# A decoder layer's softmax maxima: mask and maximum products in the two 64-row halves of the array, maxima laid out by DMAs

## What is computed

```python
scores = jnp.where(causal[None, None], scores, -jnp.inf)
attn = jax.nn.softmax(scores, axis=-1)
out = jnp.einsum('bhqk,bkhd->bqhd', attn, V).reshape(b, s, H * hd)
...
scores = jnp.where(mask == 0, jnp.asarray(NEG, dtype=scores.dtype), scores)
attn = jax.nn.softmax(scores, axis=-1)
out = jnp.einsum('bhqk,bhkd->bhqd', attn, value)
```

## Time and profile before

| what | us |
|---|---|
| median of 3 timed runs | 645.84 (641.83 to 646.57) |
| span of the profiled execution | 642.8 |
| PE busy in it | 560.4 (87%) |
| DVE busy | 522.3 (81%) |
| ACT busy | 283.7 (44%) |
| POOL busy | 237.0 (37%) |
| a steady slot (300.33 to 334.69) | 34.36 |

### The profile page before, as it was taken

How to read it: one execution, slowest core, us unless ns; L and a number is a source line. 1 busy time by engine, 2 the same in 40 slices (tenths; PEclk the granted TensorE clock), 3 DMA queues, 4 the chain that set the end, 5 groups by cost and what they waited for, 6 DMA issues and landing times.

```text
span 642.8 us, 15987 instructions
## 1 busy us (share of the span) xinstructions
PE 560.4 (87%) x5410; PEld 355.3 (55%) x5410; DVE 522.3 (81%) x1443; ACT 283.7 (44%) x671; POOL 237.0 (37%) x312
## 2 busy tenths in 40 slices
PE   4576688779989999999999998998999998887884
PEld 3344445445656576666566665565566664454543
DVE  4577867777898988989898989576989987788995
ACT  1232225445635445455454554454445454434412
POOL 5323234347124262515342525344262616232211
PEclk9988789998999999999999998998999999999999
DMA  7175453644364263536354454546262636230000
GB/s 232 32 218 152 123 137 97 196 110 130 90 182 103 81 177 92 163 91 187 84 157 121 122 155 110 161 111 170 75 179 82 163 80 178 57 112 16 24 8 25
DMA packets 75808, 76.95 MB, mean 120 GB/s; under 512 B 13056, under 2 KB 67280, under 8 KB 75728
## 3 DMA queue, kind: packets, MB, share of 16 engines
q1 hardware_dynamic: 73488, 73.58, 41.4%
q10 hardware_dynamic: 2240, 2.35, 1.2%
HBM read 39.72 MB, written 27.00 MB: 104 GB/s over the span
## 4 chain that ended last, share of the span: by engine, by line
PE 57%; DVE 20%; issue 9%; DMA 4%; POOL 4%; ACT 3%; SPq 2%; DVEq 0%; POOLq 0%; ACTq 0%
PE misc L2256 14%; PE prob L2190 7%; PE misc L2242 6%; PE xpv L2231 5%; DVE junk L1447 5%; PE score L2176 4%; PE prob L2185 4%; PE misc L2342 4%; PE misc L2284 4%; PE misc L2297 2%; DVE xden L1486 2%; PE apv L2219 2%; PE score L2152 1%; POOL move_x L728 1%; DMA xden<-xoT 1%
## 5 line engine op out<-in xcount | busy, mean ns | idle before, releaser
L1447 DVE CUSTOM_DVE_ANT_0 junk<-score,maskbias 112x375 bf16<-112x375 f32 x256 | 129.1, 543 | 38.3 <-PE score L2176 38.2
L947 ACT ACTIVATE xP<-prob 128x448 f32<-128x448 f32 (+1 forms) x192 | 93.9, 540 | 66.2 <-PE prob L2190 66.0
L728 POOL TENSOR_TENSOR move_x<-mT,negeye 16x448 bf16<-16x448 f32 x64 | 63.5, 1008 | 70.2 <-ACT mT L907 70.2
L728 POOL TENSOR_TENSOR move_a<-mT,negeye 16x448 bf16<-16x448 f32 x64 | 63.1, 1009 | 62.8 <-ACT mT L907 62.8
L2256 PE MATMUL misc<-wguT,xqT 128*128 128x352 f32 x224 | 75.0, 463 | 1.9 <-ACT xqT L907 1.1
L748 POOL TENSOR_TENSOR aattT<-anum,aden 128x224 f32<-128x224 f32 x16 | 10.9, 679 | 139.0 <-DVE aden L1486 121.1
L752 POOL TENSOR_TENSOR rstd<-veps,half 128x1 f32<-128x1 f32 (+1 forms) x44 | 28.1, 639 | 89.8 <-DVE veps L1522 89.8
L2284 PE MATMUL misc<-ctxT_s,xwkT_s 128*128 128x375 f32 x128 | 50.8, 521 | 7.9 <-DVE bq_s L1405 6.7
L2176 PE MATMUL score<-xK,xQ 64*128 64x375 f16 x256 | 43.2, 331 | 16.5 <-DVE xmax L1447 16.0
L2190 PE MATMUL prob<-move_x,shift_x 128*128 128x448 bf16 x192 | 53.7, 361 | 0.1
L2256 PEld LDWEIGHTS misc<-wguT,xqT 128*128 128x128 f32 x224 | 41.8, 190 | 21.6 <-DVE hb L1570 1.8
(11 more groups left out here) (157 smaller groups left out, 1092.2 us busy)
## 6 DMA issues: line engine op xcount, KB each, us to landing
xk_dram<-xk_parts SPq DMA_DIRECT2D x64, 192.0 KB, 3.2
xK<-xk_dram SPq DMA_DIRECT2D x16, 768.0 KB, 4.6
ctxT_s<-in_ctxT SPq DMA_DIRECT2D x15, 375.0 KB, 3.6
aq_dram<-aq_parts SPq DMA_DIRECT2D x64, 64.0 KB, 2.6
ak_dram<-ak_parts SPq DMA_DIRECT2D x64, 64.0 KB, 2.1
aQ<-aq_dram SPq DMA_DIRECT2D x16, 256.0 KB, 2.9
aK<-ak_dram SPq DMA_DIRECT2D x16, 256.0 KB, 2.9
xq_dram<-xq_parts SPq DMA_DIRECT2D x64, 64.0 KB, 2.1
```

The costliest lines, as they stand in the source:

```text
L728: pool.tensor_tensor(dst[0:H, heads, :], mT[:, n].unsqueeze(1).to_broadcast([H, GH, S]), negeye[:, heads].unsqueeze(2).to_broadcast([H, GH ...
L947: act.activation(xP[0:KEYS[c], g % 2, c], prob[m][0:KEYS[c], 0:GH * S].rearrange("p (h q) -> p h q", h=GH), ACT.Exp).then_inc(probs.taken[ ...
L1447: dve.tensor_tensor_reduce(junk[:, m], score[m][0:S, 0:SC], maskbias[:], 1.0, -3.0e38, ALU.add, ALU.max, xmax[:, b.par, h:h + 1]).then_inc ...
```

## The change

The maxima are no longer spread into a block diagonal. `amax` and `xmax` get a layout in which the four heads of a group lie at rows 0 to 3 of one half and those of the next group at rows 64 to 67, for each of two pairs of groups (`BIG`). `turn_max` turns each pair of groups by a product of its own, with 128 weight columns. ACT copies 128x224 numbers with the sign turned, as bf16. A new function `flatten` makes ACT wait for its own copy and issue two DMAs, one for each half of the array: each takes four rows of `mT` and lays them one behind another into a single row of `move` (row 0 or row 64, 1,792 bytes). The semaphores `adiag_ready` and `xdiag_ready` now count the DMAs (32 a batch), and both halves and all four groups are awaited before the first shift product.

The queries are in two sets of 56 (`j`). `shift` and `move` hold in each half of 64 rows: ones (or the maxima) in rows 0 to 3, and the mask (or the unit matrix) for the 56 queries of a set in the next 56 rows. In place of two products with 128 rows and 448 columns, `turned` issues four with 64 rows and 224 columns, of which each writes every other group of 56 columns of its bank. POOL's `diagonal` and all its calls go. `flatten` stands behind each call of `maxima` in ACT's order.

At the start the tables `move_a`, `move_x`, `amax` and `xmax` are written in the first part of POOL's preparations, ahead of the semaphore `consts` (now 24), and not behind it. The mask for `shift_x` is loaded by two DMAs into `hqT`, which POOL clears first.

```diff
@@ load_mask (SP)
-                sp.dma_start(mask_t_i[H:P, :], mask).then_inc(w_mask, 16)
+                sp.wait_ge(mask_clear, 1)
+                sp.nop(nofuse=True)
+                for a in range(2):
+                    lo = HALF * a + GH
+                    sp.dma_start(mask_t_i[lo:lo + HS].rearrange("p (j s) -> p j s", j=2),
+                                 mask.rearrange("(j q) s -> q j s", j=2)).then_inc(w_mask, 16)
@@ prep (POOL)
-                for tile in (ident, identb, causal4, shift_a, negeye):
+                pool.memset(mask_t_i, 0).then_inc(mask_clear, 1)
+                for tile in (ident, identb, causal4, shift_a, move_a, move_x):
                     pool.memset(tile[:], 0.0).then_inc(consts, 1)
+                for tile in (amax, xmax):
+                    pool.memset(tile[:], -1.0).then_inc(consts, 1)
...
+                    for move in (move_a, move_x):
+                        grid = move[rows_].rearrange("p h b j q -> p (h b j) q")
+                        pool.affine_select(out=grid, in_=grid, compare_op=ALU.not_equal, fill=1.0, base=-GH,
+                                           pattern=[[0, GH * BIG * 2], [-1, HS]], channel_multiplier=1).then_inc(consts, 1)
...
                 pool.wait_ge(diag_ready, 2)
-                pool.memset(mask_t_i[0:H], 0).then_inc(large, 1)
                 for tile in (aV, xV):
                     pool.memset(tile[:], 1.0).then_inc(large, 1)
-                for tile in (move_a, move_x):
-                    pool.memset(tile[:], 0.0).then_inc(large, 1)
-                pool.wait_ge(large, 5)
-                for tile in (move_a, move_x):
-                    pool.affine_select(out=tile[:], in_=tile[:], compare_op=ALU.not_equal, fill=1.0, base=-H,
-                                       pattern=[[0, H], [-1, S]], channel_multiplier=1).then_inc(large, 1)
-                pool.wait_ge(large, 7)
@@ POOL
-            def diagonal(i, b, g, cross):
...
-                pool.tensor_tensor(dst[0:H, heads, :], mT[:, n].unsqueeze(1).to_broadcast([H, GH, S]),
-                                   negeye[:, heads].unsqueeze(2).to_broadcast([H, GH, S]), ALU.mult).then_inc(done, 1)
@@ ACT
             def maxima(i, n, label):
                 m = miscs.wait_full(act, i, label)
-                copy(mT[:, n], misc[m][0:H, 0:S]).then_inc(miscs.taken[m], 1)
+                copy(mT[:, n], misc[m][:, 0:BIG * S].rearrange("p (g s) -> p g s", g=BIG), scale=-1.0).then_inc(miscs.taken[m], 1)
+
+            def flatten(i, n, label):
+
+                miscs.wait_taken(act, i, label)
+                act.nop(nofuse=True)
+                move, ready = ((move_a, adiag_ready), (move_x, xdiag_ready))[n]
+                for a in range(2):
+                    act.dma_start(move[HALF * a:HALF * a + 1].rearrange("p h b j q -> p h (b j q)"),
+                                  mT[HALF * a:HALF * a + GH, n].rearrange("p b s -> p (b s)")).then_inc(ready, 16)
@@ masks (DVE)
-                step(dve.tensor_scalar(shift_x[:, 0:SC], mask_t_i, 0, NEG, ALU.is_equal, ALU.mult))
-                step(dve.memset(shift_x[0:H], 1.0))
+                step(dve.tensor_scalar(shift_x[:, :, 0:SC], mask_t_i.rearrange("p (j s) -> p j s", j=2), 0, NEG, ALU.is_equal, ALU.mult))
+                for a in range(2):
+                    step(dve.memset(shift_x[HALF * a:HALF * a + GH], 1.0))
@@ turned (PE)
-                for a in range(2):
-                    g = BIG * big + a
-                    pe.wait_ge(ready, b.times(GROUPS, g + 1))
-                    pe.matmul(prob[m[a]][:, 0:GH * S], shift_[:, keys],
-                              move[:, GH * g:GH * g + GH].rearrange("p h q -> p (h q)"),
-                              start=False, stop=True).then_inc(probs.full[m[a]], 1)
+                pe.wait_ge(ready, b.times(32, 32))
+                for j in range(2):
+                    for a in range(2):
+                        rows_ = slice(HALF * a, HALF * a + HALF)
+                        mm = pe.matmul(prob[m[a]][:, 0:GH * S].rearrange("p (h j q) -> p h j q", h=GH, j=2)[:, :, j], shift_[rows_, j, keys],
+                                       move[rows_, :, big, j], start=False, stop=(j == 1))
+                        if j == 1:
+                            mm.then_inc(probs.full[m[a]], 1)
@@ turn_max (PE)
-                pe.transpose(misc[m][0:H, 0:S], mx[:, b.par], ident[0:S, 0:S]).then_inc(miscs.full[m], 1)
+                for big in range(BIG):
+                    mm = pe.transpose(misc[m][:, big * S:big * S + S], mx[:, b.par, big].rearrange("p a r -> p (a r)"), ident[0:S, 0:S])
+                mm.then_inc(miscs.full[m], 1)
```

130 lines of the change are left out of this document (44 added, 86 removed).

## The result

| | before | after |
|---|---|---|
| median of the timed runs, us | 643.84 (641.73 to 646.57, 4 runs) | 670.21 (664.85 to 673.28, 4 runs) |
| span of the profiled execution | 642.8 | 667.4 |
| granted clock of PE, mean | 0.975 | 0.948 |
| PE busy | 560.4 | 556.0 |

After takes 1.039 times as long, 95% interval 1.033 to 1.046. It lies above my range of 634 to 657: the change costs 26 us, and I had forecast no difference.

The account below looks back on a forecast made before the run. PE and DVE, both near full, bound the kernel in a loop through both. Start -3.0, ramp -0.6, ten slots +4.0 and drain -0.7 sum to -0.3 us on the 642.8 span; with 3.0 carried over, 645.5 us, range 634 to 657.

Parts of the forecast that it names:

- The steady slot: Each of ten steady slots: -0.80 shift products, +0.40 turning, +0.40 self and +0.40 cross wait, together +0.40 us.
- The sum of the shift products and turnings: PE part of a slot: five shift pairs save 0.16 each, -0.80 us; two wider turnings cost 0.20 each, +0.40.
- The first DMA's issue, 0.55: ACT's queue, after the maxima's copy: one issue takes 0.55 us, as two issues of SP take 1.10.
- From the start of the second issue to its landing 1.9: Small DMAs to `move`: 1.9 us to landing, the median for the denominators; least 1.8, most 2.3.
- at a time when DVE has no deadline: Cross case: the cross queries' high part, which DVE waits for, queues behind ACT's two issues (1.1 us) without a deadline.
- Ramp and drain: Before and after the ten slots: about 12 changed pairs count in each; ramp -0.6 us (-3 to +3), drain -0.7 (-2.5 to +1.5).
- The start: Preparations: POOL's memsets and selects stand earlier, so PE's context product comes 3.0 us earlier; ends -4.5 and +1.
- Rival 1: The small transfers are there in time: a slot is -0.40 or -0.60 us, 637 us in all; chance 0.22.
- Rival 2: Cross maxima's DMA waits behind SP's traffic at each slot's turn: slot +1.6 us, 657 us in all; chance 0.24.
- Rival 3: POOL's blocking of DVE is on the path after all: 1.26 us a slot more gained, 632 us; chance 0.07.
- Rival 4: The four shift products don't overlap and cost 0.39 us or more: slot +1.2, 654 us in all; chance 0.05.
- my own signs: Steady slot: four products in 0.19 to 0.25 us, DMA waits about 0.4, last-maximum wait 1.2, period 34.8; context product near 20.4.

Follow-up runs that it names:

- pooldiag: After's 64-row halves, start tables and wider turning, but POOL's block-diagonal products in place of the DMAs; 647.03 us, 1.0005 of the before beside it.
- noflat: After without the 64 small DMAs and PE's waits for them, maxima left out of the shift products, exponentials scaled; 632.28 us, 0.977 of before.
- spare: After with the same 64 DMAs issued by ACT into a spare tile, PE not waiting for them, maxima left out; 649.57 us.
- fill_after: After with spare products on PE before its DMA waits at five uses in ramp and drain and before the last batch's cross scores; 664.06 us.
- fill_mixed: The kernel `mixed` with 4 spare products before each pair of cross scores but the first of batches 0 and 15; 642.29 us, 0.999 of before.
- fill_before: Before with the same spare products as `fill_mixed`; 646.92 us.
- mixed: After's 64-row halves, with self maxima by one DMA per use and cross maxima by POOL's products in 4 rows; 644.34 us, 1.001 of before.
- latetab: After with the tables of `move_a` and `move_x` and the fills of `amax` and `xmax` behind the first turning; 673.78 us.
- spslot: After with the steady slots' DMAs issued by SP's queue, ramp and drain as in after; 689.43 us.
- onedma: After with one DMA of 8 rows per use in place of two, so ACT issues 32 and not 64; 647.41 us, 1.005 of before.

## Why the prediction was wrong

**The steady slot.** +0.40 forecast, +0.95 measured. The runs split it, over ten slots each, one execution per kernel:

| part | runs | forecast | measured |
|---|---|---|---|
| halves, with the wider turning | `pooldiag` - before | -0.40 | -0.38 |
| POOL's products and PE's waits for them gone | `noflat` - `pooldiag` | 0 | -0.45 |
| ACT's issues | `spare` - `noflat` | 0 | +0.53 |
| PE's waits for the DMAs | after - `spare` | +0.80 | +1.25 |

The sum of the shift products and turnings was right, though not by its parts: eight and four products end in 318.32 - 317.83 = 0.49 us where the earlier trace rows has 0.69, a gain of 0.20, but the gate products behind them hold PE for 1.39 us. Before they held it for 1.28:

```profile
310.59 0.33 PE L2176 MATMUL score<-xK,xQ 64*128 64x375 f16 x2
```

In one regular period of each kernel the DVE part is 16.67 us in `pooldiag`, `noflat`, `spare` and after alike, for 16.87 before. What splits them is the PE part, from the turning to DVE's gate operation: 17.17, 16.72, 17.37 and 18.35, for 17.49 before. Why the DVE part lost its 0.20 isn't shown; I had expected that what PE saves there only lengthens the wait of 0.76.

The step that failed first is the price of the DMA, "The first DMA's issue, 0.55" and "From the start of the second issue to its landing 1.9". The pairs of issues took 1.20 and 1.46 us, and landing after the second's start about 2.0 and 2.4: that made 0.40 and 0.40 into 0.60 and 0.97. I had let the 94% in the earlier trace rows move the cross wait from 0.17 to 0.40 only; which part of the longer issue and landing there is due to the traffic isn't shown. The second failure is "at a time when DVE has no deadline": `spare` shows PE waiting behind DVE there.

**Ramp and drain.** -0.6 and -0.7 forecast, +6.5 and +9.1 measured. This is the step on which the forecast broke: 17 of the 25 us that it missed. By the same differences of runs the ramp is +1.5 (halves), -6.8 (POOL), +9.2 (issues), +2.6 (waits), the drain +4.5, -4.0, +6.0, +2.7. Drains with the same code differ by up to 6 us, so the drain's parts are not resolved, only that it is longer. Two things were missing. I priced ACT's issues at nothing in the ramp and at less than 1 us in the drain, because ACT is half idle. The 64 issues are some 40 us of one queue; 18 of them stand in the ramp and 6 in the drain, where every engine waits for the next, and in `spare` they made the ramp 9.2 us longer with nobody waiting for the data. And I took PE's products as of fixed length. Of the 40.4 us between `noflat` and after, 16.1 are products that took longer; `fill_after` and `fill_mixed` show for one place, the last batch's gate products, that they do not when PE's idle time before them is filled. It is not shown for each place, and the ramp of `fill_before` did not answer to it.

In the drain even `pooldiag` took 4.5 us more in its profiled execution, with one wait of 0.74 for POOL: its last 8 gate products took 4.68 us against before's 2.60. Halves shorten PE's work where PE waits for DVE anyway, and it may be that what was saved came back as a lower clock; that the same eight take 2.55 in `fill_mixed` and 4.64 in `mixed` speaks for it.

**The start.** -3.0 forecast, -1.7 at the context product, which `latetab` explains: I had the mask bias start at 13.6 as in the earlier trace rows, but the mask now landed at 15.2. By the first turning only 0.5 of it is left, which is less than starts with the same code differ by. The constants at 13.4 and the first projections behind them, which I had estimated at 12 and 13.3, had slack.

**The rivals.** Rival 1, transfers in time, is `noflat` but for the issues, 5 us below its 637. Rival 2 had the right sign; its mechanism, SP's traffic, accounts for part of 0.97 us a slot in the one place, not for the loss. `spslot` is what it would look like. Rival 3, DVE freed on its path, is not what the -0.45 is: DVE's 0.89 before the gate, the 16.67 of the DVE part and PE's 0.76 for the last maximum are the same in both runs. (Its row of 0.41 "with POOL idle" overlapped a POOL product from 560.13 on; `noflat` shows 0.42.) Rival 4 falls, with a remainder: the saving is partly lost in the product that follows. I had also priced it too low, since without a saving ramp and drain lose their 1.9 each as well, which makes it +11.5 and not +8 to +9. Of my own signs the DVE operations at 0.42 came true and the start came in part. The four products take 0.30 us to the next group for 0.19 to 0.25, the waits are 0.60 and 0.97 for 0.4, the wait for the last maximum stayed at 0.76 for 1.2, DVE's idle time before the gate is 0.89 and did not grow from 0.98, and the period is 35.32 for 34.8.

## What to carry to other kernels

Price a small DMA by the queue that issues it as well as by its landing: against `noflat`, the same kernel without them, two for one use cost 38 us, one cost 15, and the issues of the two alone, with nobody waiting for the data, 17. Work out ramp and drain by their own waits and not as a remainder of the steady state: 17 of the 25 us missed were there. Moving the use of a late value back only helps if the work moved ahead of it was not the cover of another loop.

## What the hardware showed that I had not expected

- Fewer idle microseconds can be worth more than their sum: the same 5698 matmuls took 539.9, 551.3 and 556.0 us at mean granted clocks of 0.972, 0.949 and 0.948 (`noflat`, `spare`, after). With 20.9 us of spare products after's median was 6 us lower and not higher, and the last eight gate products took 2.54 us for 4.93.
- The same pair of 1.8 KB transfers reached PE 3.14 us after the first issue from ACT's queue and 4.11 us after it from POOL's, the latter in an execution with a lower clock (0.911 for 0.948); one transfer of all eight rows took 2.97 us.
- In the steady slots the issue of the single DMA (`onedma`) held ACT's queue for 0.51 to 0.53 us, and a pair of issues (after) for 1.19 to 1.34 us at the self maxima and 1.31 to 1.74 at the cross ones.
